# Attention outputs of the unmasked layers moved by transfers instead of transposes

## The reference

```python
# a: causal
attn = jnp.where(causal, einsum('bhqd,bhkd->bhqk', q, k) * scale, -inf)
a = clip(attn, -100, 100); m = max(a); e = exp(a - m)
p = e / (sum(e) + 1e-06) + 1e-08
out = einsum('bhqk,bhkd->bqhd', p / sum(p), v) @ w_proj.T
# ffn: no mask
probs = softmax(einsum('bqhd,bkhd->bhqk', q, k) * scale)
attn = einsum('bhqk,bkhd->bqhd', probs, v).reshape(B, T, D) @ Wo + bo
x = layer_norm(src + attn, ln1_g, ln1_b)
expert_idx = remainder(floor(x @ router_w + router_b), 4)   # then relu(x@W1[e]+b1[e])@W2[e]+b2[e]
```

## Time and profile before

| | |
|---|---|
| runs (3) | 2598.37 us median, 2595.04 to 2599.72 |
| profiled execution | 2579.53 us, span 2577.8 us |
| busy share of the span | PE 94%, DVE 71%, ACT 56%, POOL 52% |
| mean granted TensorE clock | 0.977 |
| rounds 0 to 15 | from 61 to some 1148 us of the span |
| rounds 16 to 23 | from 1776 to some 2300 us |

### The profile page before, as it was taken

The page is one execution under the profiler, slowest core; times in us unless marked ns, Lnnn a source line. Parts: engine busy times, 40 slices in busy tenths (PEclk is TensorE's granted clock), DMA queues, the critical chain, the costliest instruction groups (busy, mean ns, idle before and its releaser), DMA issues. The chain is left out here.

```text
span 2577.8 us, 45874 instructions
## 1 busy us (share of the span) xinstructions
PE 2418.6 (94%) x14724; PEld 1393.9 (54%) x14724; DVE 1831.9 (71%) x3685; ACT 1438.2 (56%) x2991; POOL 1351.5 (52%) x1358
## 2 busy tenths in 40 slices
PE   6999999999999999989999699988999999989998
PEld 3455555554444444349899366653344434349997
DVE  5999999999778888854333558867778888845333
ACT  3666666666777777753333232214777777653332
POOL 5356666563234554444655579843334454435655
PEclk8999999999999999999999799988999999999999
DMA  5333333333434444324665200015434444335654
GB/s 161 101 105 107 105 102 108 112 105 96 120 112 124 133 129 125 98 93 161 213 201 179 72 1 17 17 58 138 118 109 129 129 130 122 85 118 176 202 194 141
DMA packets 249936, 305.88 MB, mean 119 GB/s; under 512 B 28034, under 2 KB 224865, under 8 KB 249700
## 3 DMA queue, kind: packets, MB, share of 16 engines
q1 hardware_dynamic: 238164, 275.37, 35.8%
q0 software_dynamic: 10176, 26.27, 2.9%
q10 hardware_dynamic: 1360, 1.31, 0.2%
HBM read 210.32 MB, written 92.84 MB: 118 GB/s over the span
## 5 line engine op out<-in xcount | busy, mean ns | idle before, releaser
L783 DVE TENSOR_REDUCE neg_max_af<-sc_af 128x1 f32<-128x512 f32 (+3 forms) x864 | 551.0, 664 | 105.2 <-PE sc_af L489 101.2
L704 ACT ACTIVATE prob_af<-sct_af 128x512 f32<-128x512 f32 (+1 forms) x864 | 484.1, 582 | 234.9 <-PE sct_af L512 231.3
L783 DVE TENSOR_REDUCE neg_max_f<-sc_f 128x1 f32<-128x512 f32 x512 | 334.6, 685 | 93.0 <-PE sc_f L489 90.8
L704 ACT ACTIVATE prob_f<-sct_f 128x512 f32<-128x512 f32 x512 | 290.6, 598 | 127.5 <-PE sct_f L512 126.1
L512 PE MATMUL sct_af<-stack_q_af,stack_k_af 99*128 99x512 bf16 (+3 forms) x1024 | 320.1, 343 | 7.9 <-ACT prob_af L704 7.1
L489 PE MATMUL sc_af<-stack_k_af,stack_q_af 96*128 96x512 bf16 (+3 forms) x1024 | 320.0, 342 | 4.1 <-DVE neg_max_af L783 4.0
L1620 PE MATMUL y_ps_e<-w_r,hT_e 128*128 x1120 | 255.4, 381 | 5.7 <-issue 4.0
L812 DVE SCALAR_TENSOR_TENSOR prob_af<-prob_af,w_r 128x512 f32<-128x512 f32 (+2 forms) x224 | 233.2, 1049 | 21.7 <-ACT prob_af L704 21.5
L1807 DVE TENSOR_TENSOR y_e<-y_ps_e,b_e 128x256 f32<-128x256 f32 x70 | 29.7, 425 | 298.3 <-PE y_ps_e L1620 296.5
L540 PE MATMUL out_af<-prob_af,v_aug_af 128*32 128x512 f32 (+3 forms) x2048 | 231.9, 525 | 8.7 <-DVE prob_af L812 7.8
L1620 PEld LDWEIGHTS y_ps_e<-w_r,hT_e 128*128 128x128 f32 x1120 | 207.2, 190 | 35.3 <-issue 9.4
(11 more groups left out here) (383 smaller groups left out, 4650.0 us busy)
## 6 DMA issues: line engine op xcount, KB each, us to landing
w_r<-in_f_W_dram SPq DMA_DIRECT2D x66, 1024.0 KB, 5.1
stack_k_af<-k_parts_d SPq DMA_DIRECT2D x64, 384.0 KB, 4.3
k_parts_d<-parts_af SPq DMA_DIRECT2D x187, 128.0 KB
q_parts_d<-parts_af SPq DMA_DIRECT2D x96, 128.0 KB
stack_q_af<-q_parts_d SPq DMA_DIRECT2D x64, 192.0 KB, 2.9
stack_k_f<-k_parts_d SPq DMA_DIRECT2D x32, 384.0 KB, 4.2
w_next<-in_f_W_dram SPq DMA_DIRECT2D x12, 1024.0 KB, 4.9
k_parts_d<-parts_f SPq DMA_DIRECT2D x91, 128.0 KB
```

What stands on the lines that cost most here:

```text
L704: nc.scalar.activation(dst, src.rearrange("p (h q) -> p h q", h=len(heads)), ACT.Exp).then_inc(S.exp_done, 1)
L783: nc.vector.tensor_reduce(M.neg_max[:, qt, heads[0]:heads[-1] + 1], src, AX.X, ALU.max, negate=True).then_inc(S.max_done, 1)
```

## The change

In unmasked rounds a chunk is no longer transposed twice. Its two head groups are moved by transfers straight from `o_sb` into `attT` (`move_out`: four transfers of 16 x 512, and one that lays the four rows of sums over 64 partitions as `sums`). When both groups are moved, VectorE takes the reciprocals of `sums` (`weigh`, 128 x 32), SyncE stores them to DRAM (`store_weights`) and loads them back spread over 16 partitions a head (`spread_weights`, 128 x 512), and GpSimd multiplies the chunk by them in place (`scale_out`, 128 x 512). `attT` is doubled. This holds for 28 of 32 chunks (`by_pe` names the rest: the second chunk of the last two rounds of each pass keeps the transposes). The maxima of four query tiles go through one transpose with 48 output rows. Floor rows are made with 99 input rows, the first 96 of them zero in a new stationary tile `floor_k`. In unmasked rounds `xnT` stands in slots 10 and 11. `scatter` moves from the end of a round into the next, behind its first `split`. `add_bias` and `scale_y` run in halves of 128 x 512. Some semaphores are merged.

```diff
+    def by_pe(n, c):
+        return n < NB or (c == 1 and n % NB >= NB - 2)
...
+    def attT_uses(n):
+        if not exists(n):
+            return {}
+        if causal(n):
+            return {4: ("attT", n, 0), 7: ("attT", n, 1)}
+        return {3: ("attT", n, 1)} if by_pe(n, 1) else {}
...
+    def xnT_slots(n):
+        return (8, 11) if causal(n) else (10, 11)
...
-        elif kt == 2:
+        elif kt == 2 and by_pe(group(n, g - 1)[0], group(n, g - 1)[1] // 2):
             use = ("out",) + group(n, g - 1)
...
+            def move_out(n, g):
+                if not exists(n) or by_pe(n, g // 2):
+                    return
+                c, h = divmod(g, 2)
+                sp.wait_ge(S.o_sb, NG * n + g + 1)
+                if n > 1:
+                    sp.wait_ge(S.y_ps, 2 * (n - 1))
...
+                sp.dma_start(M.sums[64 * h:64 * h + 64, :], M.o_sb[HD:P:32, :]).then_inc(S.moved, 16)
+                for i in range(4):
+                    o = 64 * h + HD * i
+                    sp.dma_start(attT(n)[o:o + HD, c, :], M.o_sb[32 * i:32 * i + HD, :]).then_inc(S.moved, 16)
...
+                sp.wait_ge(S.weighed, chunks(n, c))
+                sp.dma_start(M.weights_d[n % NB][8 * c:8 * c + 8, :], M.weights[:, :]).then_inc(S.weights_stored, 16)
...
+                sp.wait_ge(S.weights_stored, 16 * chunks(n, c))
+                sp.wait_ge(S.moved, 80 * moved(n, 2 * c + 1))
+                if chunks(n, c) > 1:
+                    sp.wait_ge(S.out_scaled, chunks(n, c) - 1)
+                src = M.weights_d[n % NB][8 * c:8 * c + 8, :].unsqueeze(1).to_broadcast([8, HD, T])
+                sp.dma_start(M.spread[:, :], src).then_inc(S.weights_spread, 16)
...
                 load_max_rows(n, 1)
+                move_out(n - 1, 3)
                 load_res(n - 1)
                 write_parts(n + 1, 0)
+                store_weights(n - 1, 1)
                 load_stack(n + 1, 0)
+                spread_weights(n - 1, 1)
                 load_max_rows(n, 2)
+                move_out(n, 0)
...
                 load_max_rows(n, 3)
+                move_out(n, 1)
+                store_weights(n, 0)
                 load_stack(n + 1, 2)
+                spread_weights(n, 0)
...
                 elif what == "y":
-                    pe.wait_ge(S.attT_ready, 2 * n + 2)
+                    if chunks(n, 1):
+                        pe.wait_ge(S.out_scaled, chunks(n, 1))
...
-                    for t in range(KT):
-                        last = nc.tensor.transpose(Gb[0:12, t * P:t * P + P], M.max_parts[:, t, :, :].rearrange("p a h -> p (a h)"), C.ident_bf[:, :])
+                    last = nc.tensor.transpose(M.gen_bf[bank_of[use]][0:12 * KT, 0:P], M.max_parts[:, :, :, :].rearrange("p a h t -> p (a h t)"),
+                                               C.ident_bf[:, :])
...
-                nc.tensor.matmul(M.sct[u % 2][:, :], M.stack_k[96:99, g, i, 0:P], M.stack_q[96:99, g, i, :],
+                nc.tensor.matmul(M.sct[u % 2][:, :], M.floor_k[0:99, :], M.stack_q[0:99, g, i, :],
...
+            def weigh(n, c):
...
+                dve.wait_ge(S.moved, 80 * moved(n, 2 * c + 1))
...
+                nc.vector.reciprocal(M.weights[:, :], M.sums[:, :]).then_inc(S.weighed, 1)
...
                         if kt == 2:
                             normalise(pn, pg)
+                        if kt == 3 and pg % 2 == 1:
+                            weigh(pn, pg // 2)
...
+            def scale_out(n, c):
...
+                pool.wait_ge(S.weights_spread, 16 * chunks(n, c))
+                out = attT(n)[:, c, :]
+                nc.gpsimd.tensor_tensor(out, out, M.spread[:, :], ALU.mult).then_inc(S.out_scaled, 1)
...
                 lay_out_v(n, 3)
+                scale_out(n - 1, 0)
                 split(n + 1, 1)
+                scatter(n - 3)
                 split(n + 1, 2)
...
                 inv_std_x(n + 2)
+                scale_out(n - 1, 1)
                 add_floor(n, 0)
                 add_bias(n - 1)
...
-                scatter(n - 2)
+                if n == last:
+                    scatter(n - 2)
```

More of the change, by code:

```diff
@@ L72, in y_slot, with moved, outs, copies @@
         return 4 if n == end - 1 else 8
-    def attT_slots(n):
-        return (3, 4) if n == end - 1 else (4, 7)
+    def by_pe(n, c):
+        return n < NB or (c == 1 and n % NB >= NB - 2)
+    def moved(n, g):
+        return sum(1 for m in range(n + 1) for q in range(NG) if (m, q) <= (n, g) and not by_pe(m, q // 2))
+    def outs(n, g):
+        return NG * n + g + 1 - moved(n, g)
+    def copies(n, j):
+        return outs(n, 2 * j + 1) // 2
+    def chunks(n, c):
+        return moved(n, 2 * c + 1) // 2
+    def attT_uses(n):
[4 more added lines that the diff above has]
+        return {3: ("attT", n, 1)} if by_pe(n, 1) else {}
+    def attT(n):
+        return M.attT[1 if causal(n) else n % 2]
+    def att(n, g):
+        if causal(n):
+            return M.att[n % 2][:, :, 4 * HD * g:4 * HD * (g + 1)].rearrange("p t (h e) -> p t h e", h=4)
+        turned = M.attT[(n + 1) % 2][:, 0, :].rearrange("p (t d) -> p t d", t=KT)
+        return turned[:, :, 4 * HD * (g % 2):4 * HD * (g % 2 + 1)].rearrange("p t (h e) -> p t h e", h=4)
+    def att_tile(n, j, t):
+        if causal(n):
+            return M.att[n % 2][:, t, j * P:j * P + P]
+        return M.attT[(n + 1) % 2][:, 0, t * P:t * P + P]
     first_ffn = max(first, NB)
@@ L402, in bank_free @@
                     what, m, j = used_before[use]
-                    per, sem = READ_OUT[what]
-                    pe.wait_ge(sem, per * read_count(what, m) + j + 1)
+                    if what == "out":
+                        pe.wait_ge(S.out_read, outs(m, j))
+                    elif what == "attT":
+                        pe.wait_ge(S.attT_ready, copies(m, j))
+                    else:
+                        per, sem = READ_OUT[what]
+                        pe.wait_ge(sem, per * read_count(what, m) + j + 1)
             def use_bank(use, halves=(0, 1)):
@@ L1156, in scale_y @@
                     pool.wait_ge(S.key_done, i)
[L1157 removed]
+                for ts in HALVES:
+                    done = nc.gpsimd.tensor_tensor(M.prod[:, ts, :], x[:, ts, 0:D], R.rw[:, :].unsqueeze(1).to_broadcast(wide), ALU.mult)
+                done.then_inc(S.key_prod, 1)
             def link(ins):
@@ L1278, in attention_memory @@
     M.floor_v = sb("floor_v", [P, KT, 4, HD])
-    M.att = [sb(f"att{i}", [P, KT, D]) for i in range(2)]
-    M.attT = sb("attT", [P, DC, T])
+    M.sums, M.weights = sb("sums", [P, T // HD]), sb("weights", [P, T // HD])
+    M.spread = sb("spread", [P, T])
+    M.attT = [sb(f"attT{i}", [P, DC, T]) for i in range(2)]
+    o3 = o2 + 5 * D
+    M.att = [M.attT[0][:, :, :].rearrange("p c t -> p (c t)").rearrange("p (t d) -> p t d", t=KT),
+             shared[:, o3:o3 + KT * D].rearrange("p (t d) -> p t d", t=KT)]
     M.sc = [psum("sc0"), psum("sc1"), psum("sc2")]
```

183 lines of the change are left out of this document (111 added, 72 removed).

## The result

| | before | changed |
|---|---|---|
| median of the runs | 2597.07 us (4) | **2573.13 us** (4; 2568.75 to 2573.83) |
| ratio | | 0.9904, 95% interval 0.9887 to 0.9921 |
| profiled execution, span | 2579.53, 2577.8 us | 2572.77, 2571.1 us |
| busy PE, DVE, ACT, POOL | 94, 71, 56, 52% | 92, 72, 54, 54% |
| mean granted clock, profiled | 0.977 | 0.968 |

The change gains 24 us, where 76 were predicted, and 2573 lies outside the range of 2498 to 2560. In the profiles, the 24 rounds together (each last one up to the start of its slot 15) go from 1587.5 to 1564.0 us: 23.5 less. Everything else, whose code is the same, goes from 990.3 to 1007.1; a second profile of the kernel before has 1588.9 and 1002.5. So the profile that the prediction read had rounds as usual and a short time outside them. The gain in the rounds is that of the medians (23.5 and 23.9 us), so I look for the miss there.

The account below looks back on a forecast made before the run. TensorE was taken to bound unmasked rounds, TensorE and VectorE together masked ones. Terms 24.4 + 12.2 + 10.6 + 12 + 10.4 + 10 - 4 = 76 us off the median 2598.4 gave 2522 us, range 2498 to 2560.

Parts of the forecast that it names:

- Terms 1 to 3: TensorE, unmasked rounds: head-group output transposes dropped 24.4 us, chunk transposes dropped 12.2 us, maxima through one transpose 10.6 us.
- Term 4: Masked rounds: floor rows with 99 input rows and single maxima transposes gain 12 us, bounds 0 and 28.
- Term 5: Slot 8, unmasked rounds: moving input transposes away from their normalisation ends a 0.87 us stall in 12 rounds, 10.4 us.
- Term 6: Slot 2: scatter behind the first split ends ScalarE's wait for GpSimd's shift in ten rounds, 10 us; bound 0.
- GpSimd's list: GpSimd's unmasked round: splits done 22.2, spreading load down 22.5, ready 24.1, half a us of slack; 4 us charged.
- rival E: Shared SBUF access: 24 added GpSimd passes each hold VectorE once, at most 28 us lost, 2550 us; chance 0.03.
- A: Unmasked rounds: GpSimd becomes pacemaker, router's sum late, 24 to 48 us lost, 2546 to 2570 us; chance 0.15.
- B: Unmasked rounds, slots 11 to 15: freed TensorE time runs into VectorE, gain 55 us, 2543 us; chance 0.10.
- C: Way through DRAM late, delaying bias, router's sum and projection; break-even at a landing near 30; slower than before; chance 0.04.
- D: Whole kernel: no change, because of a bound not seen in the rows; chance 0.02.

Follow-up runs that it names:

- masked_gate: last_free plus, in masked rounds, GpSimd waiting for the maxima split at the end of slot 15 before the first split of parts: 2520.0 us, ratio 0.973 to before.
- xnT_back: free_split with the input's transposes of unmasked rounds back in slots 8 and 11: 2541.1 us, ratio 0.9805 to before.
- scatter_back: Changed kernel with only the row scatter back at the head of the round, ahead of GpSimd's shift: 2554.1 us, ratio 0.9882 to before.
- free_split: Changed kernel with earlier weight store and spreading load, scatter transfers over the first maxima split, GpSimd waiting for the second, router's sum asked one slot later: 2537.1 us, ratio 0.9787.
- last_free: free_split plus, in each pass's last round, GpSimd waiting for the maxima split at the end of slot 3 before the bias: 2528.2 us, ratio 0.9761.
- gate: Changed kernel with only waits added: GpSimd waits for the maxima split before its third split of parts and before the bias: 2596.6 us, ratio 1.005.

## Why the prediction was wrong

The terms of TensorE were about right. In masked_gate, which keeps every part of the change, the rounds take 76.1 us less than before (1587.5 to 1511.4): 15.6 in masked ones, 50.2 in the 14 unmasked, 10.2 in rounds 15 and 23. That this is the predicted 76 is partly luck: 8.6 us of it are falls of the clock that the kernel before had (10.3 less 1.7), and some 3 us are holds that it had in slot 4 of rounds 15 and 23; neither was in the sum. Point by point:

- **Terms 1 to 3.** Right where a slot shows them alone. Slots 6 and 14 went from 4.15 and 4.05 to 3.71 and 3.68 us; slots with the maxima take 3.98, forecast 3.97. 48 rows still pay the way in and out, as I took it.
- **Term 4**, 12 us of the masked rounds. Right in size, not in time: 556.9 to 550.9, only 6 us, came. Less the falls of the clock they go from 550.0 to 538.2, 11.8 us. The other 6 went to the clock, which fell eight times, 12.7 us instead of 6.9. A part of what TensorE was freed of turned into waits for VectorE: slot 1 of rounds 1 to 6 went from 4.51 to 5.08 us, slots 12 and 13 from 3.66 and 3.99 to 3.96 and 4.24.
- **Term 5**, 10.4 us. Right in size: from before to masked_gate slots 8 and 10 together lost 1.17 us, less 0.44 of output transposes 0.73, in 14 rounds 10.2 us. The step given for it is half of it: moving the transposes is worth 0.47 us in a full round, 5.8 us in all (xnT_back). The other half went with ScalarE's copy of `attT` ahead of the normalisation, which I had listed as lost work and not followed to this wait.
- **Term 6**, 10 us. The stall of slot 2 did go. Less its 0.44 us of output transposes, slot 2 lost 0.39 us in each of 14 rounds and 1.2 in rounds 15 and 23 (5.16 to 3.49), 8 us in all. But I named nothing that the scatter would hit in its new place. It moved the second pair of splits onto the end of slot 3, which cost 16 us there (scatter_back).
- **GpSimd's list.** Up to the third split it was right within 0.3 us (forecast 22.2, measured 21.9). Then "the spreading load of 256 KB behind the score stacks is down by 22.5": it was issued at 24.6, and GpSimd had it at 30.0. The five transfers of `move_out` ahead of the stores of parts, 3.1 us of issuing, and six stores of parts that took 6.0 us to issue, where the earlier trace rows have 3.63, put the store of the weights at 18.4 instead of 15; the stacks' load waits for those same stores, and the spreading load stood behind it. I had said what follows if this comes past 24.1, and gave it 0.04. The router's sum still waited only 1.0 us (L1008 in round 12), as the held VectorE came to it late itself.
- **The step that failed** is the one under rival E: "the added ones do not stand beside the splitting of maxima". They did not have to stand there; together with the moved scatter (end of slot 3, scatter_back) and the late load (end of slot 7) they pushed the passes that were there before onto it, at both places. And E's price was capped at "once, for at most its own length". In fact up to four steps in a chain wait for one pass each. Held time rose by 34 us (20.7 to 54.7), and the rounds are 36 us shorter in free_split, where the holds are gone from the 14 rounds; 8.6 of these are fewer falls of the clock. E had a chance of 0.03; it was the main case. The Trainium skill's SBUF — State Buffer (Who interferes with whom) says that a VectorE instruction with two SBUF inputs, or a cast in a two-port mode, contends with GpSimd under an exclusive lock for a whole instruction, and `tensor_reduce` never. The rows agree in which steps are held: L892 to L898 are, and L880 at 883.52, 0.69 us, is not; in which mode the casts ran no row shows.
- **The clock.** I made no term for it. In the rounds it cost 15 us more than before, some of it behind these very waits. That is the second missing term.

The shortfall of 52.6 us in the rounds, taken to masked_gate (76.1 less 23.5), splits: 36.4 from changed to free_split (33.1 in the 14 rounds, 3.4 in masked ones), 9.2 to last_free, 7.0 to masked_gate. Seen the other way, 23.8 of it are falls of the clock by the count above (25.5 less 1.7) and the other 28.8 are waits. Not all of it is the change's own: rounds 15 and 23 had a shorter hold before it. Rivals: A did not come by itself, but gate shows its price. B: no, VectorE is busy 51.8 of 62.6 us once it is not held. C: the landing was at its break-even of 30, but it cost by the passes, not by the projection. D: no.

The range's lower end, 2498, is 2 us below what its own terms give (2522 - 16 - 6 = 2500); nothing hangs on it.

What stays open: outside the rounds all twelve profiles with the changed parts have 998 to 1011 us, and the two of the kernel before 990 and 1002. Whether the rest costs a few us more is not settled by two profiles. Nor is it shown what makes the clock fall: gate has the longest waits and the most falls, masked_gate hardly any falls with waits left, and no run sets the cause apart.

## What to carry to other kernels

When work is moved on GpSimd, write down where each of its passes will stand against VectorE's short instructions from SBUF, in time and not only in sum; a chain of k such steps under back-to-back passes cost up to k pass lengths here. Put transfers' issues over the chain instead, or let GpSimd wait for the chain, where who needs its result can wait too. And time that TensorE is freed of next to an engine that is nearly full can turn into waits, and the clock fell behind some of these: count it with less than its full size.
